# Output products of a head group's last query tile moved into the instruction order of the next head group

## The reference, cut to what matters

```python
q = (x @ wq).reshape(b, s, H, HD); k = (x @ wk).reshape(b, s, KV, HD); v = (x @ wv).reshape(b, s, KV, HD)
q, k = apply_rope(q, cos, sin), apply_rope(k, cos, sin)
scores = jnp.einsum('bqhd,bkhd->bhqk', q, k) / np.sqrt(HD)        # causal mask
probs = jax.nn.softmax(scores, axis=-1)
out = jnp.einsum('bhqk,bkhd->bqhd', probs, v).reshape(b, s, H * HD)
return out @ wo                                                    # h = hidden + this
```

## Time and profile before

| what | value |
|---|---|
| median of 3 runs | 1355.61 us (1352.35 to 1356.25) |
| the profiled execution's own time | 1357.88 us |
| its span | 1356.1 us, 18606 instructions |
| granted TensorE clock, mean over the span | 0.925 |
| first attention, about | 14 to 441 us |
| second attention, about | 746 to 1181 us |
| busy: PE, PE weight load, DVE, ACT, POOL | 87%, 72%, 70%, 57%, 44% |

### The profile page before, as it was taken

How to read it: one execution, slowest core, us unless ns; L and a number is a source line. 1 busy time by engine, 2 the same in 40 slices (tenths; PEclk the granted TensorE clock), 3 DMA queues, 4 the chain that set the end, 5 groups by cost and what they waited for, 6 DMA issues and landing times.

```text
span 1356.1 us, 18606 instructions
## 1 busy us (share of the span) xinstructions
PE 1174.1 (87%) x6576; PEld 976.2 (72%) x6576; DVE 955.6 (70%) x1799; ACT 773.1 (57%) x1510; POOL 599.1 (44%) x450
## 2 busy tenths in 40 slices
PE   5799999999999499963398799999999999849994
PEld 4688788788787378851277578878878878638883
DVE  6677677777787757748757667777777778757774
ACT  5666566666564167742453656656666656417772
POOL 3664575575610034521412375466476370004541
PEclk9899999999999589995789799999999989859998
DMA  4100100100000941124100200010010000193113
GB/s 126 36 0 2 35 1 1 35 1 1 1 1 1 318 159 51 51 81 144 51 1 1 66 1 1 1 36 1 1 36 1 1 1 1 40 347 103 51 52 117
DMA packets 48651, 66.29 MB, mean 49 GB/s; under 512 B 5808, under 2 KB 34352, under 8 KB 48432
## 3 DMA queue, kind: packets, MB, share of 16 engines
q1 hardware_dynamic: 42032, 50.94, 11.5%
q0 software_dynamic: 4416, 12.06, 2.9%
q10 hardware_dynamic: 2112, 2.10, 0.4%
HBM read 54.86 MB, written 10.22 MB: 48 GB/s over the span
## 4 chain that ended last, share of the span: by engine, by line
PE 80%; DVE 11%; ACT 3%; DMA 2%; POOL 2%; issue 2%; SPq 0%; DVEq 0%; POOLq 0%; ACTq 0%
PE ps L1375 21%; PE ps L1377 19%; PE ps L1376 19%; PE ps L1444 9%; PE ps L1505 6%; PE ps L1493 2%; PE ps L1432 1%; POOL probs L681 1%; DVE h L1079 1%; DMA xs<-rows_dram,token_of 1%; PE ps L1513 1%; PE ps L1476 1%; PE ps L1347 1%; DVE negmax L1058 1%; DVE mixT L1309 1%
## 5 line engine op out<-in xcount | busy, mean ns | idle before, releaser
L748 ACT ACTIVATE probs<-ps,negmax 128x128 f32<-128x128 f32 (+7 forms) x256 | 189.6, 741 | 109.2 <-DVE negmax L1058 106.9
L754 ACT ACTIVATE probsT<-ps 128x512 fp32r<-128x512 f32 x288 | 168.6, 597 | 135.6 <-PE ps L1444 133.4
L1058 DVE TENSOR_REDUCE negmax<-ps 128x1 f32<-128x128 f32 (+7 forms) x256 | 191.2, 751 | 64.0 <-PE ps L1432 62.0
L1063 DVE TENSOR_TENSOR probsT<-ps,probsT 128x512 fp32r<-128x512 f32 x288 | 195.0, 686 | 44.7 <-ACT probsT L754 42.8
L1444 PE MATMUL ps<-square,probs 128*128 128x128 f32 x1152 | 170.1, 275 | 5.9 <-DVE values L1053 5.9
L652 POOL DMA_INDIRECT xs<-rows_dram,token_of x46 | 68.5, 1489 | 214.3 <-DVE token_of L1154 181.8
L608 POOL TENSOR_TENSOR crossed<-crossed,rope 128x512 f32<-128x512 f32 x70 | 91.5, 1308 | 161.3 <-ACT crossed L735 161.3
L1079 DVE SCALAR_TENSOR_TENSOR h<-ps,rowinv,h 128x256 f32<-128x256 f32 x256 | 123.2, 481 | 48.5 <-PE ps L1377 36.1
L1444 PEld LDWEIGHTS ps<-square,probs 128*128 128x128 f32 x1152 | 134.1, 141 | 25.7 <-DVE values L1053 6.2
L1375 PE MATMUL ps<-keysT,queriesT 128*128 128x512 f32 (+3 forms) x384 | 141.2, 368 | 9.1 <-ACT probs L748 4.3
L1162 DVE TENSOR_TENSOR parts<-experts,parts 128x1024 fp32r<-128x1024 f32 x92 | 112.2, 1225 | 49.7 <-ACT parts L794 49.2
(11 more groups left out here) (229 smaller groups left out, 2897.7 us busy)
## 6 DMA issues: line engine op xcount, KB each, us to landing
experts<-in_L_ffn_w_dram SPq DMA_DIRECT2D x48, 512.0 KB, 10.5
w_in<-in_L_ffn_wq_dram SPq DMA_DIRECT2D x8, 512.0 KB, 3.9
wo_in<-in_L_ffn_wo_dram SPq DMA_DIRECT2D x8, 512.0 KB, 6.3
rows_dram<-probs ACTq DMA_DIRECT2D x4, 512.0 KB, 10.1
probs<-y_dram SPq DMA_DIRECT2D x8, 256.0 KB, 4.2
mixT<-y_dram SPq DMA_DIRECT2D x8, 256.0 KB, 4.7
probs<-in_L_attn_x_dram SPq DMA_DIRECT2D x2, 512.0 KB, 4.5
w_in<-in_L_ffn_wk_dram SPq DMA_DIRECT2D x8, 128.0 KB, 4.7
```

The costliest lines, as they stand in the source:

```text
L748: act.activation(probs[:, i % 2, k, 0:w], ps[:, 2 * slot_n:2 * slot_n + 2, :].rearrange("p b n -> p (b n)")[:, 0:w], ACT.Exp, bias=negmax[ ...
L754: act.activation(probsT[:, m % 3, 0, :], ps[:, 4 + m % 2, :], ACT.Copy).then_inc(S["probsT_high"], 1)
L1058: dve.tensor_reduce(negmax[:, m:m + 1], ps[:, s:s + 2, :].rearrange("p b n -> p (b n)")[:, 0:w], AX.X, ALU.max, negate=True).then_inc(S["m ...
L1063: dve.tensor_tensor(probsT[:, m % 3, 1, :], ps[:, 4 + m % 2, :], probsT[:, m % 3, 0, :].bitcast(F32), ALU.subtract).then_inc(S["probsT_low ...
```

## The change

The steps `attn_high`, `attn_low`, `out` and `added` of the last query tile (i = 7) leave the order of their own group, in all groups but the last of an attention. They come in as the steps of tile -1 of the next group's order. There they are planned among the first steps of that group, with due times of tile -1. They keep their buffers (-1 % 2 = 1, -1 % 4 = 3), their semaphore counts and their weights, and `h[:, i]` becomes `h[:, i % NT]`. In the plan, `values(1, 0)` and `max(3, 0)` come after `added(-1, 1)`, and `wo_split` comes after `out(-1, 1)`. On PE `values(0, 0)` and `values(1, 0)` get a wait for the additions two tiles back in groups 1 to 3. Pool's code is not changed. No instruction is added or removed besides these waits.

```diff
-def group_order(more, opening=False):
+def group_order(more, opening=False, carry=False):
...
-    add("Pool", ("wo_split", 0, 0), 4.4, 0)
+    def project_out(i):
+
+        add("ACT", ("attn_high", i, 0), 0.52, i + 1.2, ("values", i, i), ("attn_high", i - 1, 0), ("out", i - 2, 1))
+        add("DVE", ("attn_low", i, 0), 0.75, i + 1.2, ("attn_high", i, 0), ("attn_low", i - 1, 0))
+        for k in range(2):
+            add("PE", ("out", i, k), 0.64, i + 1.3 + 0.2 * k, ("attn_low", i, 0), ("added", i, k - 1), ("out", i - 1, 1),
+                ("wo_split", 0, 0))
+            add("DVE", ("added", i, k), 0.95 if more or not k else 1.4, i + 1.3 + 0.2 * k, ("out", i, k), ("added", i, k - 1), ("added", i - 1, 1))
+
+    if carry:
+        project_out(-1)
+        later += [(("values", i, 0), ("added", -1, 1)) for i in (1,)] + [(("max", 3, 0), ("added", -1, 1))]
+    add("Pool", ("wo_split", 0, 0), 4.4, 0, ("out", -1, 1))
...
+        if i < NT - 1 or not more:
+            project_out(i)
...
-        ORDERS = {more: group_order(more)[0] for more in (True, False)}
+        ORDERS = {more: group_order(more, carry=True)[0] for more in (True, False)}
...
-                        if k == 0:
-                            if i >= 2:
-                                pe.wait_ge(S["out_added"], REP * (NT * gg + i - 1))
+                        if k == 0 and (g or i >= 2):
+                            pe.wait_ge(S["out_added"], REP * (NT * gg + i - 1))
```

More of the change, by code:

```diff
@@ L1078, in group @@
                                 dve.wait_ge(S["out_added"], REP * (NT * gg + i) + hd)
-                            dve.scalar_tensor_tensor(out=h[:, i, :], in0=ps[:, 6 + i % 2, (hd % 2) * D:(hd % 2 + 1) * D],
-                                                     scalar=rowinv[:, m + hd:m + hd + 1], in1=h[:, i, :],
+                            dve.scalar_tensor_tensor(out=h[:, i % NT, :], in0=ps[:, 6 + i % 2, (hd % 2) * D:(hd % 2 + 1) * D],
+                                                     scalar=rowinv[:, m + hd:m + hd + 1], in1=h[:, i % NT, :],
                                                      op0=ALU.mult, op1=ALU.add).then_inc(S["out_added"], 1)
-                        if k == 1 and order is ORDERS[False]:
+                        if k == 1 and order is ORDERS[False] and i >= 0:
                             dve.wait_ge(S["out_added"], REP * (NT * gg + i + 1))
```

## The result

| | before | after |
|---|---|---|
| median | 1355.93 us (6 runs, 1350.81 to 1356.83) | 1372.90 us (6 runs, 1370.65 to 1374.20) |
| profiled execution, its span | 1357.88, 1356.1 | 1374.20, 1372.4 |

What follows compares the result with a forecast made beforehand. PE was taken as the bound, busy 96.22 of a group's 98.65 us. New stalls of 4.5 less 2.32 removed, taken as 2.3 at six boundaries, plus 1.4, made +15.2 us: median 1370.8, range 1361 to 1377.

Steps and rivals of the forecast that it cites:

- The two waits of 1.15 and 1.17 us: PE's waits before the two out steps ending a group; removing them gains 2.32 us at each of six boundaries.
- The order: The step sequence on PE and DVE at the group's head, worked out by the greedy rule with due times.
- The first stall: PE before values(1,0), which waits for added(-1,1) at the end of DVE's queue: 1.1 us, bounds nothing to 1.8.
- The second: PE idle after scores(2,3), waiting for straight(q1,1) to free a slot: 1.4 us, bounds 0.7 to 1.6.
- The third, Pool: Pool's w_o split, 2.65 us later, delays q1,0 and crossed(q1,2); PE waits 1.7 us before scores(3,1), bounds 1.1 to 2.7.
- The sum: Per boundary, new stalls of 4.5 us less 2.32 removed; taken as 2.3 us net, 13.8 for six.
- smaller stalls: Further new PE stalls at a boundary, not named singly: about 0.3 us together.
- extra wait for exp(9,3): At the boundary of groups 0 and 1, scores(2,0) waits for exp(9,3)'s slot: 0.7 us counted, twice, 1.4.
- The faster one: Rival: the two waits at each group's end are filled and nothing replaces them, 1341.7 us; chance 0.15.
- The draw: Rival: DVE's queue and straight(q1,1) eat the gain, Pool's lateness is covered, 1357 us (1353 to 1360); chance 0.13.
- The worse one: Rival: Pool's lateness also hits scores(4,3), or the order packs less densely, 1377 to 1383 us; chance 0.08.

Runs made afterwards that it cites:

- run 9: Kernel before, with out(7,1) written to PSUM bank 6 instead of 7 and no step moved: 1343.4 us, ratio 0.9919.
- run 10: Kernel before, boundary rewritten on PE and DVE, with out(-1,1) in PSUM bank 6 right behind out(-1,0): 1337.6 us, ratio 0.9879.
- run 2: Kernel after, with the additions of tile -1 into h cut from 256 columns to 32: 1378.7 us.
- run 1: Kernel after, with Pool's split of w_o moved behind block q1,0, as in the plan: 1360.0 us, ratio 1.0037.
- run 4: Kernel before, with only Pool made late by extra work ahead of its split of w_o in three groups of each attention: 1365.2 us, ratio 1.0078.
- run 5: Kernel after, with eight steps moved on PE, DVE and ACT, Pool left late: 1381.0 us, ratio 1.0202.
- run 8: Kernel before, with the boundary order rewritten on PE and DVE, ACT and Pool as before: 1350.1 us, ratio 0.9970.
- run 7: Kernel before, with only PE's order at the boundary rewritten: 1356.6 us, ratio 1.0023.
- run 3: Kernel after, with Pool's split behind block q1,0 and the additions of tile -1 cut to 32 columns: 1357.9 us, ratio 1.0026.
- run 6: Kernel after, with eight steps moved on PE, DVE and ACT, and Pool's split behind block q1,0: 1355.1 us, ratio 1.0017.

## Why the prediction was right

- **What bounds the kernel, and what is removed.** Right. The two waits of 1.15 and 1.17 us go, and runs 9 and 10 show that they can be had for good: 2.3 us a boundary. What I had said of all six boundaries, that they look alike, does not hold: at the one at 1085 us the granted clock falls, as told below.
- **The order.** The order that I followed is the one in the trace, on PE and on DVE, for all the steps listed. The whole sum hangs on it.
- **The first stall.** Size right (1.1 predicted, 1.24 measured), reason only in part. I put it down to DVE's queue of eight operations. The trace and run 2 show that the pair of additions itself is 1.00 us of it and the handing over from PE to DVE and back 0.24, since values(1,0) stands right behind out(-1,1). It is the old wait of 1.17 us again, one step later. DVE was through with the operations ahead of the additions just when PE ended, so they added nothing. My DVE chain and PE's stream ended within 0.1 us of each other, so either would have given the number: that part is luck.
- **The second.** Right: 1.4 predicted, 1.42 measured, for `straight`, once a group.
- **The third, Pool.** Right in mechanism and about right in size (1.7 predicted, 1.53 measured), and shown from both sides: run 1 takes it away from the kernel after, run 4 puts a like one into the kernel before (0.94 us of wait at that place, and 1.9 us a group in all). What I had not said is that it is an anchor. While Pool is late, nothing that PE and DVE save ahead of it counts (runs 2, 5).
- **The sum.** 2.3 us a boundary predicted, 2.6 measured in groups 1 and 2. Only 1.86 us of it is waiting: 4.19 for the three stalls less 2.33 for the two. The 0.3 us that I gave to smaller stalls is not there as waiting. What stands in its place, and in that of the rest, is that PE is busy longer with the same matmuls (96.90 instead of 96.22 us). Matmuls overlap, and around a wait they overlap less: the first one of values(1,0) begins 0.31 us before the next, the following ones 0.23 (run 9 has the same from the other side, 1.30 us for a wait of 1.17). Another thing that the sum lacked is group 3: its order is planned with other costs, and beside the three stalls PE waits there 1.05 us for an exponential and 0.43 us for `low`. The first of these goes too when Pool is released (run 1). The two group-0 boundaries have their extra wait for exp(9,3), 0.67 us measured against 0.7.

```profile
377.66 0.50 PE L1383 MATMUL ps<-keysT,queriesT 128*128 128x512 f32 x1 [1.05 <-ACT probs L756]
```

- **Luck in the total.** In its second attention the profiled execution of before lost clock behind its two waits, from just before 1087 us on, and the one after did not. The same steps, from the first out(7,0) of group 2 to that of group 3, in the first and the second attention of before:

```profile
348.11:436.68 88.57, 85.59 (x516) 70.57 (x517) 70.93 (x127) 51.74 (x101) 25.00 (x18) 1.00 0.00 1
1085.18:1176.05 90.87, 88.14 (x517) 72.82 (x517) 69.90 (x127) 51.75 (x101) 25.07 (x18) 0.96 0.00 1
```

That is 2.3 us which the second execution did not lose and I had not seen, about as much as group 3 took and I had not seen either (1.5 us in each attention). The stretch between the attentions, which the change does not touch, was 1.4 us shorter as well: from the first `square,probs` matmul behind the first attention (443.25, then 453.21) to the first `keysT,queriesT` of the second (768.65, then 777.23) it took 325.4 and 324.0 us. The median came out 2 us from the forecast with terms missing on both sides.
- **The rivals.** The faster one fell for the planned order and holds for one written by hand. The Trainium skill, Perfetto Trace Analysis, Optimization Strategy, says that interleaving regimes may improve performance; here the runs agree only when the queues of the other engines go along: 1.0138 as planned, 1.0023 with PE alone, 0.9970 with PE and DVE, 0.9879 with Pool released too by another bank. That bank alone gives 0.9919, so the interleaving itself brings 0.3% (run 8) to 0.4% (run 10 beside run 9). The draw fell with run 1. The worse one did not come in groups 1 and 2, where scores(4,3) does not wait; in group 3 the order did pack less densely, by the 1.5 us named above.

## What to carry to other kernels

When steps are moved on one engine, list every queue that waits for the last of them, the idle ones first: here Pool, free for 38 us of a group, had 0.7 to 1.5 us of slack in the one place that counted. A stall that ends only when another engine gets through absorbs whatever is saved ahead of it, so mend the anchor first and judge the others after it. And ask of a wait whether it is for data or for a place: for a place, another buffer took it away with nothing moved.

## What the runs showed of the hardware that I had not expected

The granted clock of TensorE falls from full (2.4 GHz) to half (1.2 GHz) behind some stalls that are only 1 to 4 us long in a stream that is busy without a gap otherwise, and this makes a stall cost more than its length. Of the six boundaries of a profiled execution it fell at

| PE's waits at a boundary | boundaries with a fall |
|---|---|
| one of 3.99 to 4.05 us (run 5) | 6 |
| 0.78 and 1.42, then one of 2.01 us (run 2) | 4 |
| one of 1.88 us (run 7) | 5 |
| 1.16 and 1.17 us, 1 us of matmuls between them (before; run 4) | 1; 2 |
| 1.24, 1.42 and 1.53 us, about 4 us of matmuls between them (after) | 0 |
| the waits of runs 1, 3, 6, 8, 9 and 10, none above 1.51 us | 0 |

A fall cost 1.25 us (run 2) to 1.3 us (run 7), and 2.3 us in the kernel before, where the clock was low for 6 to 7 us and not for 3.5. In run 4 it fell in group 2 of both attentions (mean clock 0.98 over that group in the first, 100.74 us). The rows of the kernel before:

```profile
1087.00:1088.00 1.00, 0.67 (x3) 0.68 (x4) 0.27 (x1) 0.00 (x0) 0.00 (x0) 0.50 0.00 0
...
1092.00:1093.00 1.00, 1.00 (x4) 0.71 (x4) 0.12 (x1) 0.23 (x2) 1.00 (x1) 0.50 0.00 0
```

The executions of the kernel before took 1350.8 to 1360.6 us, with a mean clock of 0.930 and 0.923 at these two; whether such falls make that difference no trace shows. The Trainium skill, TensorE: Matmul & The Clock Gate, HAM oscillation, says that waits between bursts of matmuls can throttle PE again and again. The traces agree for runs 5 and 7, with a fall at six and five of six boundaries. Why the same two waits bring it down at one boundary and not at the five others no run here tells.
